# Splitting the dummy transposes ahead of a selective scan: 24 in an earlier-free bank, 30 behind the first two pairs

## What is computed

```python
delta = softplus(einsum('dr,brl->bdl', dtproj_w, x_dbl[:, :r]) + dt_bias[None, :, None])
dA = exp(einsum('bdl,dn->bdln', delta, A))
dBx = einsum('bdl,bnl,bdl->bdln', delta, Bm, u)
h = _ssm_scan(dA, dBx)               # h[l] = dA[l] * h[l-1] + dBx[l]
y = einsum('bdln,bnl->bdl', h, Cm)
y = y + Dp[None, :, None] * u
```

## Time and profile before

| | |
|---|---|
| Time, median of 3 runs | 370.71 us (370.65 to 370.89) |
| Time of the profiled execution | 371.32 us |
| Span of the profiled execution | 369.5 us |
| Mean granted TensorE clock | 0.927 |
| Busy: PE, DVE, ACT, POOL | 310.6, 289.4, 247.4, 204.3 us |

### The profile page before, as it was taken

One profiled execution on the slowest core, in us unless ns is written; L12 is line 12 of the kernel. 1 busy time (PEld: TensorE's weight loads), 2 busy tenths in 40 slices (PEclk: granted clock), 3 DMA queues, 4 the chain that ended last, 5 costly groups with the idle time before them and its releaser, 6 DMA issues.

```text
span 369.5 us, 5605 instructions
## 1 busy us (share of the span) xinstructions
PE 310.6 (84%) x1757; PEld 191.3 (52%) x1757; DVE 289.4 (78%) x475; ACT 247.4 (67%) x452; POOL 204.3 (55%) x142
## 2 busy tenths in 40 slices
PE   6999697999999998999999999888999763089940
PEld 5444494565556544445454547535666552078820
DVE  2869789999999999999999994796899547212532
ACT  3579978999999989999999984746767610022200
POOL 6501468999999988998889850200000023700374
PEclk9999969999999999999999999999999965559985
DMA  6996211223232331333221000000000000240000
GB/s 159 315 260 229 64 58 59 81 92 114 77 121 89 114 115 63 108 116 113 77 97 57 1 0 2 1 2 0 2 2 0 3 0 17 64 108 2 15 29 14
DMA packets 15377, 26.22 MB, mean 71 GB/s; under 512 B 1972, under 2 KB 8909, under 8 KB 15349
## 3 DMA queue, kind: packets, MB, share of 16 engines
q1 hardware_dynamic: 14580, 24.76, 21.4%
q0 software_dynamic: 768, 1.11, 1.0%
HBM read 23.49 MB, written 2.51 MB: 70 GB/s over the span
## 4 chain that ended last, share of the span: by engine, by line
PE 42%; DVE 29%; POOL 10%; issue 10%; ACT 5%; DMA 2%; POOLq 0%; SPq 0%; DVEq 0%; ACTq 0%
DVE arena L1171 21%; PE bank L698 19%; POOL arena L438 5%; PE bank L742 4%; PE bank L923 3%; DVE acc L1181 3%; PE bank L840 3%; PE bank L1042 3%; PE bank L1052 2%; PE bank L764 2%; POOL out L488 2%; PE bank L942 2%; ACT arena L659 2%; POOL dispatched_tokens L469 1%; PE bank L730 1%
## 5 line engine op out<-in xcount | busy, mean ns | idle before, releaser
L438 POOL TENSOR_TENSOR arena<-arena,k_maskT 128x1024 f32<-128x1024 f32 x64 | 150.5, 2377 | 37.7 <-DVE arena L1158 19.7
L1171 DVE TENSOR_TENSOR_SCAN arena<-bank,arena 128x512 f32<-128x512 f32 x128 | 146.0, 1199 | 0.0
L698 PE MATMUL bank<-ident,arena 128*128 128x128 f32 x716 | 106.2, 282 | 30.2 <-DMA arena<-dispatched_tokens 12.7
L698 PEld LDWEIGHTS bank<-ident,arena 128*128 128x128 f32 x716 | 77.8, 141 | 99.3 <-DVE arena L1171 55.7
L840 PE MATMUL bank<-conv_in_T,ident 128*128 128x512 f32 x192 | 92.8, 593 | 0.0
L551 ACT ACTIVATE bank<-delta,a_neg 128x508 f32<-128x508 f32 x128 | 88.3, 692 | 6.6 <-DVE arena L1171 5.8
L595 ACT ACTIVATE conv_in_T<-bank,c_col 128x256 f32<-128x256 f32 x192 | 80.4, 473 | 12.5 <-PE bank L698 11.7
L450 POOL TENSOR_SCALAR rstd<-moments 128x4 f32<-128x4 f32 (+3 forms) x5 | 1.3, 252 | 75.1 <-DVE moments L1223 75.1
L495 ACT ACTIVATE arena<-bank 128x512 f32<-128x512 f32 (+3 forms) x32 | 13.2, 436 | 41.8 <-PE bank L1032 31.8
L840 PEld LDWEIGHTS bank<-conv_in_T,ident 128*128 128x128 f32 x192 | 31.6, 191 | 15.8 <-issue 15.0
L1181 DVE SCALAR_TENSOR_TENSOR acc<-bank,c_col,acc 128x256 f32<-128x256 f32 x64 | 27.3, 467 | 1.8 <-PE bank L698 1.6
(11 more groups left out here) (168 smaller groups left out, 338.1 us busy)
## 6 DMA issues: line engine op xcount, KB each, us to landing
k_maskT<-b_rows SPq DMA_DIRECT2D x32, 512.0 KB, 3.7
w_sb<-in_L_ffn_w SPq DMA_DIRECT2D x1, 2048.0 KB, 11.2
dispatched_tokens<-zeros SPq DMA_DIRECT2D x1, 650.0 KB, 18.8
x_tok<-in_x SPq DMA_DIRECT2D x1, 512.0 KB, 3.9
ctx_tok<-in_ctx SPq DMA_DIRECT2D x1, 512.0 KB, 3.8
out<-uT SPq DMA_DIRECT2D x1, 512.0 KB, 3.9
arena<-dispatched_tokens SPq DMA_DIRECT2D x2, 130.0 KB, 2.2
arena<-dispatched_tokens SPq DMA_DIRECT2D x1, 260.0 KB, 3.5
```

The source lines that it names most:

```text
L438: gp.tensor_tensor(dBx[g % 2][h], du[:, dr, h, :], b_bc[:, g % RING, :], ALU.mult).then_inc(dBx_ok, 1)
L698: return pe.transpose(dst, src, ident[0:src.shape[0], 0:src.shape[0]])
L1171: ve.tensor_tensor_scan(o, a, v, 0.0, ALU.mult, ALU.add).then_inc(scanned, 1)
```

## The change

Three edits. The list `held_at_scan` keeps one entry more, so that it holds the last holder of bank 5. The 50 dummies into bank 3, behind the wait for the read of `skip`, become 24 dummies into bank 5, behind the wait for the read of `d100`; the wait for `skip` stands behind them. And 30 dummies into bank 5 follow the first two pairs of step 0.

```diff
@@
             if n == scan_from:
-                held_at_scan, holder = holder[0:Y_BANK], [None] * Y_BANK + holder[Y_BANK:]
+                held_at_scan, holder = holder[0:Y_BANK + 1], [None] * Y_BANK + holder[Y_BANK:]
@@
+            wait_read(pe, held_at_scan[Y_BANK])
+            keep_busy(Y_BANK, 24)
             wait_read(pe, held_at_scan[HT_BANK])
-            keep_busy(HT_BANK, 50)
             for g in range(STEPS):
                 pe.wait_ge(scanned, 4 * g + 2)
                 for b in (0, 2):
                     turn_pair(g, b)
+                if g == 0:
+                    keep_busy(Y_BANK, 30)
                 if g:
                     add_part(g - 1, 1)
                     add_part(g - 1, 2)
```

## The result

| | kernel before | changed kernel |
|---|---|---|
| Median, 9 runs of each | 370.79 us (370.01 to 371.51) | 373.23 us (372.33 to 374.94) |
| Ratio | | 1.0072, 95% interval 1.005 to 1.0095 |
| Profiled execution: time, span | 371.32, 369.5 us | 374.5, 372.8 us |

The changed kernel is slower by 2.4 us by the medians and by 2.7 us by the ratio, 0.7%. The ratio is worked out from the single runs and is not the quotient of the two medians.

The account below looks back on a forecast made before the run. The scan stage was taken to run at DVE's pace, with one 1.6 us wait for TensorE. Pairs 4 and 6 2.9 us later, less 0.3 recovered, tail 0: 370.71 + 2.6 = 373.3 us, range 370.3 to 374.6.

Parts of the forecast that it names:

- pairs 4 and 6: Step 0's last turns on TensorE, behind the second batch: to start 2.9 us later than before (bounds 0.1 and 3.6).
- the sums of step 1: DVE's sums in the scan stage, at 61.20 before: pair 0 of step 1 ready at 63.4, 2.2 us later.
- what is recovered: Scan stage: TensorE's idle ahead of pair 0 and loop slack give back 0.3 us, chosen between 0 and 0.56.
- The wait for d111: TensorE idles 2.5 to 4.5 us until 54.35, as pair 2 needs bank 4 read; clock then at half.
- The second batch: 30 turns ahead of pairs 4 and 6, mostly at half clock, over at 60.9 (bounds 58.1 and 61.6).
- Three of the signs: Changed profile: 30 turns take 5.5 us or more, DVE's next sums not before 63, second DVE wait about 3 to 4 us.
- Where the lateness goes: DVE's sums of step 1 come 2.2 us late, the rest after the next skip step; scan stage ends 2.6 us later.
- Rival A: Clock stays full across the wait for d111, batch ends at 58.1: about 370.5 us, no measurable change; chance 0.22.
- Rival B: Dummies never warm the second batch, which ends at 61.6: 3.3 us slower, 374.0 us; chance 0.07.
- Rival C: DVE's lead of 1.62 us is kept to the end, needing the second batch over at 57.1: 369.1 us; chance 0.06.
- the gain at the sums: Step 0: DVE's sums start at 54.31, not 55.93, 1.62 us earlier, for one step only.
- the tail: Start of the expert stage may meet the clock's rise earlier or later: 0 taken, 1.4 us either way as bound.

Follow-up runs that it names:

- the swap with 44: Changed kernel with the banks of d101 and d111 swapped and 44 dummies in the second batch, not 30: 369.71 us, 0.9988 times the kernel before.

## Why the prediction was right

**The number.** Predicted 373.3, measured 373.23; the agreement to a tenth is luck, as the second pair of profiles shows. Of the terms, first profile against first profile: pairs 4 and 6 start 2.92 us later (60.91 for 57.99; predicted 2.9), the sums of step 1 2.09 us later (2.2), step 3 2.54 us and the end of the scan stage 2.55 us later (2.6). The choice of 0.3 us for what is recovered, which had no row, measured 2.92 - 2.55 = 0.37.

**The wait for d111** was as predicted, in both profiles: 3.7 us of idle, ended by DVE's L1146, with the clock down inside it (from 53.3 and from 53.8). Filling the wait, or moving it with two banks swapped, takes the loss away: shown.

**The second batch** took 5.65 us (predicted 5.7) and 4.26 us in the second profile. The 5.9 us of work until the clock rises, taken from one row, fitted the first profile (from 54.4 to a rise at 60.1) and not the second (a rise at 57.2, 2.9 us behind 54.3). Three of the signs that the prediction named also held in the first profile alone: a batch of 5.5 us or more, sums not before 63 (61.88 in the second), and a wait of 3 to 4 us (2.34). The forecast stood all the same because the batch of 50 in the kernel before was shorter by 1.2 us in its second profile too: pairs 4 and 6 start 2.92 us later in the first pair of profiles and 2.74 us in the second (59.51 for 56.77). No term of the prediction says that the two would move together; that part is luck. That the second batch costs by its speed and not just by its place is shown by the kernel with 30 dummies more. That place counts too is shown by the kernel before with 30 more: 1.4 us at full clock.

**Where the lateness goes.** The trace has DVE's waits of 3.73 and 0.46 us just where they were put, at the first sums after the batch and at the first after a skip.

**Rival A** (full clock across the wait, about 370.5) did not happen in either profile of the changed kernel, and no run of it was under 372.33. But four profiles have the same code up to pair 2, those two and the ones with 15 and with no dummies behind, and in the one with 15 the clock was full at 54.35, as rival A needs; it fell 1.1 us later. So the clock at that date differs from one execution to the next, and full clock there does not keep the batch at full clock. With the clock kept up by more dummies, the time was 371.77, a ratio of 1.0023 (1.0008 to 1.0038), and not the 370.5 without a change that A had. Its first claim, that the lead of DVE is lost in the skip steps when TensorE starts no earlier, holds: the lead over the first profile of before was 0.68 us at step 1 (60.52 for 61.20) and 0.23 at step 3 (71.57 for 71.80). **Rival B** (never warm) did not happen. **Rival C** (the lead kept) needed the batch over by 57.1; it ended at 60.9, and at 59.5 in the second profile.

**What was wrong in it.** First, the gain at the sums was priced as 1.62 us from one execution; another has 0.41 there. The forecast didn't hang on it, since TensorE's lateness and not DVE's lead set the end, but every expectation of 369.1 did: two of the three missed by about a microsecond (370.34 and 370.11), the one early batch of 50 by 2.7. Second, the tail got 0 with 1.4 us either way as a property of the kernel. It is one of the execution: the time from the first turn of the expert stage to the end of the span was 45.57 and 46.38 us in the two profiles of before and 46.27 and 45.53 in those of the changed kernel, longer where the clock rose later behind that turn (8.8, 10.4, 10.1 and 8.6 us). In the means of the two profiles it is level (46.0 and 45.9 us), and the median followed the 2.55 us of the scan stage and not the 3.3 us of the first pair of spans. Third, idle times of 2.61 and 3.77 us were read as long enough to lose the clock and 1.66 us as not; the last section has 2.58 us after which it did not fall, and 3.97 us at whose end it was still full.

**Open.** The median of the kernel with one early batch of 50, 0.2% above before, is not explained by its one profile, in which the scan stage is early. Its twelve runs reach from 370.07 to 372.74 us. The clock's fall just ahead of pairs 4 and 6 may come in more or in less of them; with one profile of that kernel this was not counted.

## What to carry to other kernels

Dummy work that keeps the clock up belongs inside a wait of TensorE, where what stands behind it on the queue could not start yet anyway: with 30 turns behind pair 2 the kernel was 2.4 us slower than before, with the same 30 ahead of pair 2 it was level with it. Before splitting a batch that is "only filler", look up which waits it hid: here a bank read that ended at 54.3 and that no wait in the profile of before shows, because the batch ended at 55.3. And don't price a gain of a microsecond from one execution when the clock changes near it; take two profiles of the kernel before.

## What the runs showed of the hardware

The changes of the clock are not tied to the program's start. Over thirteen profiles, whose code is the same up to 43 us but for the two bank numbers of the swap, the first fall lay at 41.3, 41.8, 42.0, 45.6, 45.8, 46.0, 46.1, 46.4, 46.5, 46.9 and twice at 47.0 us. In the thirteenth, the swap with 44, the clock did not fall in this region at all, though TensorE idled 2.58 us (stretches, 0.00 us busy and then the batch):

```profile
43.20:45.60 2.40, 0.00 (x0) 1.00 0.55 217
45.70:49.00 3.30, 2.84 (x24) 1.00 0.00 0
```

An idle time of 2.61 us, on the other hand, is what it fell in near the end of the kernel before. And in the profile with 15 dummies behind pair 2, 3.97 us of idle ended with the clock still full; it fell at 55.4, when TensorE had been at work for 1.1 us. In the second profile of the changed kernel it fell at 47.0, 1.3 us into a batch without a gap. So the length of an idle time alone does not say whether the clock falls, nor does it always fall inside one. In the profile without a second batch it fell at 41.3, between these two stretches, while the records show small turns and then the skip matmuls; the only idle time among TensorE's work from 38.65 on is one of 0.21 us, ahead of 39.55:

```profile
40.50:41.20 0.70, 0.70 (x13) 1.00 0.18 35
41.50:43.20 1.70, 1.70 (x10) 0.50 0.00 0
```

The dates differ in the two profiles of each kernel, and with them the end of the scan stage, by 1.2 us before and 1.4 us changed, and the time from the first turn of the expert stage on, by 0.8 and 0.7 us. The kernel before took from 369.26 to 371.57 us in 34 runs on one chip; that the dates of the clock account for all of that spread is not shown. The Trainium skill says in "TensorE: Matmul & The Clock Gate", Part 1 (What's actually happening), that the hardware's watch on TensorE's activity runs freely and is not reset when a kernel starts. The first falls above, at 41.3 to 47.0 us under the same code, agree with that.
